# A vision tower on one Trainium2 core: other pieces for the last reads, clock-keeping products spread over the tail, patch weights centred by the vector engine, a shorter routing index

## The chip, the cores and the metric

The kernel runs on one core of one Trainium2 chip. The metric is the time of one execution on the device in microseconds (us), the median of several runs. One core has a matrix engine (PE; the loading of its stationary operand is shown as PEld), a vector engine (DVE), a scalar engine (ACT), a general engine (POOL) and a queue engine (SP), and 16 DMA engines that all queues share. Each engine executes its own instruction list in order; between engines there are only semaphores.

## The reference

16 images of 3x96x96 become 36 patches of 768 values each; with a class token there are 37 tokens an image and T = 592 tokens of width 256.

```
tokens = patches @ W.T + b                     # 768 -> 256
h  = concat([cls, tokens], axis=1) + pos
x  = layernorm(h) * g1 + b1                    # causal attention with low-rank q, k, v, out; 16 heads
h1 = h + attention(x);  a = h1 + mlp(layernorm(h1) * g2 + b2)
h  = layernorm(h + a)
logits = h @ gate.T; scores = softmax(logits); w, idx = top_k(scores, 3); w = w / sum(w)
y  = sum over the 3 chosen experts of w * fc2_e(gelu(g) * x * mult)      # 15 experts
ys = the shared expert of 512 hidden units, for every token
out = layernorm(h + y + ys)
```

A layer normalisation doesn't see a constant that is added to all features of a token, so the kernel keeps the token vectors centred (mean over the 256 features taken off).

## The kernel before, in words

Everything is float32 and features lie on partitions (2 chunks c of 128), tokens on the free axis in two halves n of 296. All orders are written out by hand: each engine has a block in which its instructions stand as they execute.

**Start.** SP issues six transfers `embed_sb<-embed` (L433), one for each chunk k of 128 of the 768 patch values; one holds the weights (`tw_sb`, 256 columns) and the patches (`pt_sb`, 576 columns). PE first multiplies zeros (`keep_clock`, `fill`: products that nobody reads, which keep it busy), then does the 24 products of the embedding into four PSUM banks. DVE adds bias and position while it takes them out into `h0` (L915). PE then multiplies `h0` by a matrix of 1/256 (`mean`, L1425), DVE subtracts those means (`centre`, L925) into `xc`, and ACT squares `xc` for the variance (`squares`, L668). `bias_means` and `centre_biases` do the same for the biases of attention output and MLP (`vec_sb`). After that PE composes the low-rank q, k and v weights (`compose`), one after the other, between the steps of the normalisation. POOL meanwhile takes the first bias row off expert weights (`less_first`, L407), which wait for their transfers, and then stages keys for the attention scores (`keys_block`, L372), for which PE waits before `scores(0)`.

**Attention, MLP.** Eight pairs of images through a software pipeline, then the low-rank MLP. The change doesn't touch them.

**Routing, during the shared expert.** The shared expert is eight units k = 0 to 7. In each, PE makes two products (`h,stage`), ACT a gelu (L821), DVE the gated product (L1336, semaphore `t1_done`), and PE two units later the down product (`xn,stage`). After its gated product of unit k DVE does a part of the routing, `routing(k)`: top 3 (`select`), places of the tokens in their experts (`order`, `slots`, from the product `positions` of PE), the chosen slots (`choose`, L1198 to L1261), one-hot tables (`groups_hot`, `places_hot`, L1281), the owners of slots (`owners`), and from PE's `slot_table` (15 products, `128x63`) the index lists for gathering and scattering (`tables`, L1301 to L1308). POOL waits for `gather_i` and then gathers token rows for 21 tiles of 128 rows (L635); PE waits for the first of them (`tile_transposed`, L1798).

**Experts and tail.** 21 tiles go through two products; POOL scatters the rows of each tile to `y_dram` (L644), a row of 1 KB each, to a place worked out from token and choice: for a group of 32 tokens the 96 rows of their three choices lie together, group after group (19 groups). When the last scatter has landed SP reads them back in five transfers (`read_rows`, L421): partition p = 32*choice + token, four groups each, one row of 1 KB for each partition and group. While this goes on, PE puts bias and residual into five PSUM banks (`b_sb,comb` and `cst_sb,hs`), then multiplies zeros 8 times, then for t = 0 to 4 waits for read t (`ld_y[t]`) and sums with the `mix` weights (`wres,embed_sb`). DVE and ACT normalise tile t (L1395 to L1408, L870, L875) and SP stores it (L532).

```
            for t in range(TT):
                pe.wait_ge(ld_y[t], 16)
                for j in range(min(PC, NSUM - PC * t)):
                    ...
```

Of the kernel before, what the change touches and what calls it, by code (L numbers as in the profile page):

```python
# [82 lines left out]
YROWS = NT * P + KS * NSUM  # L83
# [3 lines left out]
RT_END = 28  # L87
# [33 lines left out]
C_DST, C_DUMP = _col(TOPK * TT), _col(NT)  # L121
NRTE = _v


def vit_tower_kernel(nc, embed, vecs, csts, vrows, ut, out_u, out_v, fc1_u, fc1_v, fc2_u, fc2_v,
                     gate, shared, experts, mults, bias1, rtes, b2, out, comb_dram, x_dram, y_dram):
    ctx = ExitStack()
    with ctx:
# [22 lines left out]
        h0 = h0_mem[:, :].rearrange("p (c t) -> p c t", c=DC)  # L151
# [39 lines left out]
        res_b = sb("res_b", [P, DC, 2])  # L191
        w_sum = sb("w_sum", [P, 3])

# [49 lines left out]
        pick_i = sb("pick_i", [P, 2, TOPK * TT], I32)  # L243
# [24 lines left out]
        owner = pt_mem[:, 0:(NOVER) * E].rearrange("p (i e) -> p i e", e=E)  # L268
# [22 lines left out]
        def column(i):  # L291
# [6 lines left out]
        ld_emb = [sem(f"ld_emb{k}") for k in range(KP)]  # L298
        ld_cst, ld_vec, ld_out = sem("ld_cst"), sem("ld_vec"), sem("ld_out_w")
# [34 lines left out]
            sem(n) for n in ("mask_done", "pos_mm", "comb_done", "route", "hot_done", "pick_done"))  # L334
        own_done, tab_mm, tab_out, idx_done = sem("own_done"), sem("tab_mm"), sem("tab_out"), sem("idx_done")
# [20 lines left out]
        mean_mm, centred_h0, w_cen = (sem(n) for n in ("mean_mm", "centred_h0", "w_cen"))  # L356
# [74 lines left out]
        def _(sp):  # L431
            for k in range(KP):
                sp.dma_start(emb[:, k], embed[:, k]).then_inc(ld_emb[k], 16)  # L433
# [64 lines left out]
            for k in range(TOPK):  # L498
                at = NT * P + KS * (NSUM - 1) + SUMS * k
                sp.dma_start(y_dram[at + SUM_LAST:at + SUMS, :], zrow[0:SUMS - SUM_LAST, :]).then_inc(st_zero, 16)  # L500
# [163 lines left out]
        def _(act):  # L664
            def squares(ln, n, src, made, each):
                for c in range(DC):
                    act.wait_ge(made, DC * n + c + 1 if each else n + 1)
# [24 lines left out]
            squares(ln1, 0, xc[:, 0], centred_h0, False)  # L692
            squares(ln1, 1, xc[:, 1], centred_h0, False)
# [98 lines left out]
            for g in range(NH * FIC):  # L792
# [3 lines left out]
                if g == 1:  # L796
                    squares(ln2, 1, half(h1, 1), op_done, True)
                if g == 11:
                    squares(ln3, 0, half(hs, 0), mo_done, True)
            warm(ACT.Sqrt)  # L800
            squares(ln3, 1, half(hs, 1), mo_done, True)
# [1181 lines left out]
```

## Time and profile before

| what | value |
|---|---|
| median of 3 runs | 218.86 us (218.07 to 219.18) |
| the profiled execution, its own time | 218.37 us |
| its span, first to last instruction | 216.6 us |
| mean granted PE clock, share of full | 0.982 |
| PE busy | 202.2 us, 93% of the span |
| DVE, ACT, POOL busy | 106.7, 94.4, 120.4 us |
| read from memory, written | 29.25 MB, 4.06 MB |

The time is 1.8 us more than the span, for what lies before the first and after the last instruction. Busy PE time counts products in flight, so 93% doesn't mean that the array is full. In the profile "idle 0.52 <-DMA x" says that an engine stood idle for 0.52 us and that x ended it.

### The profile page before, as it was taken

To read this page: it belongs to the slowest core of one execution; us is meant where nothing else is said; L and a number is where in the kernel's file an instruction comes from. 1 tells how busy PE (TensorE), PEld (TensorE's weight loads), DVE (VectorE), ACT (ScalarE), POOL (GpSimd) and SP (SyncE) were. 2 spreads that over 40 slices of the span, in tenths; PEclk is the share of its full clock that TensorE was granted. 3 is DMA by queue.
4 is the path that set the end of the run, shared out by engine and by line. 5 is a ranking of instruction groups with operands and counts; after the bars stand their busy time and mean duration, and the time that the engine had idled before them with its cause. 6 is when DMAs were issued, how large, how long until landed. Compare 5 with 4: busy or idle time off the path is not lost.

```text
span 216.6 us, 4391 instructions
## 1 busy us (share of the span) xinstructions
PE 202.2 (93%) x1551; PEld 128.4 (59%) x1551; DVE 106.7 (49%) x295; ACT 94.4 (44%) x219; POOL 120.4 (56%) x148
## 2 busy tenths in 40 slices
PE   7999899989998899989999999899999999998952
PEld 4777577667886675756877763354444555445510
DVE  4076587748973444275579943523334222230044
ACT  2003543568868373553438672233323333324023
POOL 0040099649979867949998077407756652257000
PEclk9999999999999999999999999999999999999975
DMA  6999999920000299941021023319975321112692
GB/s 220 396 394 351 410 420 419 414 113 5 6 3 3 78 381 369 420 111 48 3 98 30 0 73 102 99 33 339 371 275 193 92 73 53 48 48 98 166 229 88
DMA packets 15054, 38.30 MB, mean 177 GB/s; under 512 B 2713, under 2 KB 6298, under 8 KB 15034
## 3 DMA queue, kind: packets, MB, share of 16 engines
q1 hardware_dynamic: 13018, 32.53, 41.7%
q0 software_dynamic: 2016, 5.51, 8.2%
q8 instruction: 13, 0.21, 0.4%
q14 instruction: 7, 0.06, 0.1%
HBM read 29.25 MB, written 4.06 MB: 154 GB/s over the span
## 4 chain that ended last, share of the span: by engine, by line
PE 81%; DVE 6%; DMA 6%; ACT 2%; issue 1%; POOL 1%; SPq 1%; POOLq 0%; DVEq 0%; ACTq 0%
PE ps L364 70%; DMA wres<-y_dram 3%; PE ps L1798 3%; PE ps L1609 2%; PE ps L1838 2%; PE ps L1622 2%; DMA embed_sb<-embed 2%; DMA y_dram<-ln_mem,dest_i 1%; PE ps L1542 1%; POOL y_dram L644 1%; DVE ln_mem L990 1%; DVE nw_i L974 1%; DVE nw L979 1%; DVE nw L980 1%; SPq L421 1%
## 5 line engine op out<-in xcount | busy, mean ns | idle before, releaser
L364 PE MATMUL ps<-wres,cT 128*64 (+1 forms) x360 | 62.9, 468 | 1.7 <-DVE cT L1363 0.6
L364 PEld LDWEIGHTS ps<-wres,cT 128*64 128x64 f32 (+1 forms) x360 | 25.5, 131 | 29.4 <-issue 22.2
L644 POOL DMA_INDIRECT y_dram<-ln_mem,dest_i x21 | 20.7, 985 | 27.3 <-ACT ln_mem L852 24.0
L407 POOL TENSOR_TENSOR wres<-wres,fac_mem 128x512 f32<-128x512 f32 x22 | 27.2, 1272 | 2.9 <-DVE ln_rs L981 2.9
L635 POOL DMA_INDIRECT embed_sb<-x_dram,gather_i x21 | 20.4, 971 | 13.5 <-DVE gather_i L1303 6.5
L1356 DVE TENSOR_TENSOR h<-ps,h 128x256 f32<-128x256 f32 x21 | 8.1, 420 | 33.0 <-PE ps L1838 24.9
L846 ACT ACTIVATE h<-ps 128x256 f32<-128x256 f32 x21 | 8.1, 384 | 30.1 <-PE ps L364 30.1
L364 PE MATMUL ps<-h,stage 128*128 128x296 f32 x64 | 18.0, 419 | 0.0
L852 ACT ACTIVATE ln_mem<-ps 128x256 f32<-128x256 f32 x21 | 8.1, 384 | 16.4 <-PE ps L364 16.4
L1363 DVE COPY cT<-ps 128x256 f32<-128x256 f32 x21 | 8.8, 423 | 10.3 <-PE ps L364 8.7
L364 PEld LDWEIGHTS ps<-h,stage 128*128 128x128 f32 x64 | 11.7, 190 | 3.7 <-issue 0.4
L553 POOL TENSOR_TENSOR wres<-wres,cst_sb 128x111 f32<-128x111 f32 x32 | 10.9, 373 | 5.1 <-PE ps L1622 5.1
L407 POOL TENSOR_TENSOR wres<-wres,hs 128x512 f32<-128x512 f32 x4 | 5.6, 1429 | 13.7 <-DMA wres<-experts 13.7
L364 PE MATMUL ps<-xn,wres 128*128 128x296 f32 x48 | 13.1, 419 | 0.0
L789 ACT ACTIVATE embed_sb<-ps,vec_sb 128x296 f32<-128x296 f32 x16 | 8.1, 505 | 10.6 <-PE ps L364 10.4
L364 PE MATMUL ps<-embed_sb 128*128 128x288 f32 (+1 forms) x63 | 12.5, 357 | 0.1
L364 PEld LDWEIGHTS ps<-embed_sb 128*128 128x128 f32 (+1 forms) x63 | 9.6, 168 | 3.3 <-DMA embed_sb<-embed 0.7
L364 PE MATMUL ps<-embed_sb,f1v 128*128 128x296 f32 x32 | 10.9, 429 | 0.6 <-DVE embed_sb L1099 0.5
L372 POOL TENSOR_TENSOR wres<-wres,cst_sb 128x148 f32<-128x148 f32 x16 | 10.2, 660 | 1.3 <-PE ps L364 1.3
L678 ACT ACT_TABLE_LOAD x8 | 10.3, 1283 | 1.2 <-DVE eps_t L887 1.1
L364 PEld LDWEIGHTS ps<-xn,wres 128*128 128x128 f32 x48 | 8.8, 190 | 3.2 <-issue 0.5
L364 PE MATMUL ps<-embed_sb,f2u 128*128 128x296 f32 x32 | 10.5, 416 | 0.0
(208 smaller groups left out, 379.4 us busy)
## 6 DMA issues: line engine op xcount, KB each, us to landing
wres<-experts SPq DMA_DIRECT2D x15, 768.0 KB, 13.4
fac_mem<-experts SPq DMA_DIRECT2D x11, 256.0 KB, 8.1
embed_sb<-embed SPq DMA_DIRECT2D x6, 416.0 KB, 5.2
wres<-ut SPq DMA_DIRECT2D x3, 768.0 KB, 8.9
stage<-shared SPq DMA_DIRECT2D x2, 771.0 KB, 16.4
wres<-y_dram SPq DMA_DIRECT2D x4, 384.0 KB, 5.7
stage<-wres SPq DMA_DIRECT2D x2, 512.0 KB
f1v<-fc_v SPq DMA_DIRECT2D x1, 512.0 KB
```

Of the source, the lines that this page charges most:

```text
L364: return nc.tensor.matmul(o, w, x, start=start, stop=stop)
L372: return eng.tensor_tensor(kblk[:, par, u, c], kT[:, c, bass.ds(p * (2 * S) + u * S, S)].unsqueeze(1).to_broadcast([P, HR, S]), cst[:, C_B ...
L407: nc.gpsimd.tensor_tensor(w1(e, c), w1(e, c), row, ALU.subtract).then_inc(less_done, 1)
L553: pool.tensor_tensor(vst[:, par, c, u].rearrange("p (r s) -> p r s", r=G3), vT[:, c, bass.ds(p * (2 * S) + u * S, S)].unsqueeze(1).to_broa ...
L635: pool.indirect_dma_start(out=xg[:, i % NXG], out_offset=None, in_=x_dram[:, :], in_offset=bass.IndirectOffsetOnAxis(ap=gather_i[:, column ...
L644: pool.indirect_dma_start(out=y_dram[:, :], out_offset=bass.IndirectOffsetOnAxis(ap=dest_i[:, column(i):column(i) + 1], axis=0), in_=ys[:, ...
L678: nc.scalar.activation(warm_t[:, i:i + 1], eps_t[:, 0:1], function)
L789: nc.scalar.activation(hm[:, f], ps[:, HM_BANK + g % 2, 0:HT], ACT.Gelu_apprx_tanh, bias=vec[:, C_FC1B + f:C_FC1B + f + 1]).then_inc(hm_do ...
L846: nc.scalar.activation(gel_r[:, i % 2], ps[:, 4 + i % 2, F:2 * F], ACT.Gelu).then_inc(ge_done, 1)
L852: nc.scalar.activation(ys[:, i % NYS], ps[:, i % 2, 0:D], ACT.Copy).then_inc(ys_done, 1)
L1356: nc.vector.tensor_tensor(a_r[:, i % 2], ps[:, 4 + i % 2, 0:F], gel_r[:, i % 2], ALU.mult).then_inc(a_done, 1)
L1363: nc.vector.tensor_copy(aT[:, i % 2].rearrange("p f s -> p (f s)"), ps[:, 2 + i % 2, 0:F]).then_inc(at_done, 1)
```

## The change

1. **Patch weights centred.** The transfer of chunk 0 is split in two (weights, then patches). DVE takes the mean over the 256 features off the weights of each chunk, in place, in two instructions (`centre_chunk`: a sum and a scaled subtraction), before PE may use the chunk (`tw_cen`). Position, class token and biases are gathered in `place_b`, centred together (`bias_means` now between chunks 3 and 4, 39 columns), and the embedding is taken out of PSUM straight into `xc`. `h0` as a result, `mean` and `centre` are gone. `squares` waits for each chunk of the half.
2. **Routing.** `choose` works on slot numbers times 64 by operations with two tensor operands and moves from unit 3 to unit 2, ahead of the gated product of unit 3; everything behind it moves a unit up. PE does `positions` before the down product of unit 0 and `slot_table` before unit 6 instead of unit 7; `tables` comes before `owners`.
3. **Last reads.** The rows of `y_dram` lie so that the 20 groups of one partition are together. Each of the five reads is now one run of 4 KB on each of 96 partitions (3 KB in the last). The places follow from two tables and a factor of 20 in `tables`.
4. **Unread products.** Instead of 8 at one place, 2 after each of the five residuals and 3 before each sum but the first.

```diff
-            for k in range(KP):
+            sp.dma_start(tw_sb[:, 0], embed[:, 0, 0:D]).then_inc(ld_emb[0], 16)
+            sp.dma_start(pt_sb[:, 0], embed[:, 0, D:EC]).then_inc(ld_pt, 16)
+            for k in range(1, KP):
                 sp.dma_start(emb[:, k], embed[:, k]).then_inc(ld_emb[k], 16)
...
+            def centre_chunk(k):
+                dve.wait_ge(ld_emb[k], 16)
+                nc.vector.tensor_reduce(tw_sum[:, k:k + 1], tw_sb[:, k], AX.X, ALU.add).then_inc(tw_cen, 1)
+                dve.wait_ge(tw_cen, 2 * k + 1)
+                nc.vector.scalar_tensor_tensor(tw_sb[:, k], tw_sum[:, k:k + 1].to_broadcast([P, D]), -1.0 / D,
+                                               tw_sb[:, k], ALU.mult, ALU.add).then_inc(tw_cen, 1)
...
-                    nc.vector.scalar_tensor_tensor(
-                        hv[:, n * HB:(n + 1) * HB, 1:S],
+                    nc.vector.tensor_tensor(
+                        by_image(xc[:, n, c])[:, :, 1:S],
                         ps[:, 2 * n + c, 0:HP].rearrange("p (b s) -> p b s", b=HB),
...
-            centre(0)
-            centre(1)
-            centre_biases()
...
-                pe.wait_ge(ld_emb[k], 16)
+                if k == KP - 2:
+                    bias_means()
+                pe.wait_ge(tw_cen, 2 * k + 2)
...
-            mean(0)
-            mean(1)
-            bias_means()
...
-                nc.vector.tensor_copy(place[:, :, :], pick_i[:, :, :]).then_inc(rt, 1)
-                nc.vector.tensor_scalar(upper[:, :], place[:, 0], NT - 0.5, float(TM), ALU.is_ge, ALU.mult).then_inc(rt, 1)
+                nc.vector.scalar_tensor_tensor(upper[:, :], pick_i[:, :], NT * TM - 0.5, tm_t[:, :],
+                                               ALU.is_ge, ALU.mult).then_inc(rt, 1)
...
                 if k == 2:
                     order()
                     slots()
+                    choose()
                 if k == 3:
-                    choose()
+                    groups_hot()
...
                 if k == 6:
-                    pe.wait_ge(rt, 9)
+                    pe.wait_ge(idx_done, 1)
+                    pe.wait_ge(tab_out, 2)
...
+        y_sums = y_dram[NT * P:YROWS, :].rearrange("(p c) d -> p c d", p=KS)
-            eng.dma_start(yr[:, lo:hi],
-                          y_dram[NT * P + KS * lo:NT * P + KS * hi, :].rearrange("(c p) d -> p c d", p=KS)) \
-                .then_inc(ld_y[t], 16)
+            eng.dma_start(yr[:, lo:hi], y_sums[:, lo:hi]).then_inc(ld_y[t], 16)
...
-            keep_clock(2, 8)
+                keep_clock(2, 2)
             pe.wait_ge(mix_done, TOPK * PC)
             for t in range(TT):
+                if t:
+                    keep_clock(2, 3)
                 pe.wait_ge(ld_y[t], 16)
```

How the instructions stand at three places. First the start of PE (all of its products go through one helper line, L364 before and L374 in the change). Before:

```order
L364 MATMUL ps<-fill 128x296 x12
L364 MATMUL ps<-embed_sb 128x288 x24
L364 MATMUL ps<-h,ones_t 128x296 x4
L364 MATMUL ps<-vec_sb,ones_t 128x2 x2
L364 MATMUL ps<-wres,cT 32x256 x12
L364 MATMUL ps<-ln_mem,ones_t 32x74 x8
```

And with the change:

```order
L374 MATMUL ps<-fill 128x296 x12
L374 MATMUL ps<-embed_sb 128x288 x16
L374 MATMUL ps<-place_b,ones_t 128x39 x2
L374 MATMUL ps<-embed_sb 128x288 x8
L374 MATMUL ps<-wres,cT 32x256 x12
L374 MATMUL ps<-ln_mem,ones_t 32x74 x8
```

The four products of 296 columns for the means are gone, and the product for the biases stands inside the embedding.

Second, PE in units 2 to 7 of the shared expert, from the product of `positions` with the triangle to the first expert tile. `mask` belongs to `positions`, `128x63` is `slot_table`. Before:

```order
L364 MATMUL ps<-xn,stage 128x296 x2
L364 MATMUL ps<-mask,tri_bf 128x90
...
L364 MATMUL ps<-xn,stage 128x296 x2
L364 MATMUL ps<-embed_sb 128x63 x15
L364 MATMUL ps<-h,stage 128x296 x4
L364 MATMUL ps<-xn,stage 128x296 x6
L1805 TENSOR_LOAD owner_i
```

With the change:

```order
L374 MATMUL ps<-mask,tri_bf 128x90
...
L374 MATMUL ps<-embed_sb 128x63 x15
L374 MATMUL ps<-h,stage 128x296 x4
L374 MATMUL ps<-xn,stage 128x296 x2
L374 MATMUL ps<-h,stage 128x296 x4
L374 MATMUL ps<-xn,stage 128x296 x6
L1833 TENSOR_LOAD owner_i
```

`positions` stands one down product earlier and `slot_table` one whole unit earlier.

Third, the end of PE: residuals, unread products (`fill`), sums. Before:

```order
L364 MATMUL ps<-b_sb,comb 80x256
L364 MATMUL ps<-cst_sb,hs 80x128 x2
L364 MATMUL ps<-fill 128x296 x8
L364 MATMUL ps<-wres,embed_sb 32x256 x18
L364 MATMUL ps<-wres,embed_sb 16x256
```

With the change:

```order
L374 MATMUL ps<-b_sb,comb 80x256
L374 MATMUL ps<-cst_sb,hs 80x128 x2
L374 MATMUL ps<-fill 128x296 x2
L374 MATMUL ps<-wres,embed_sb 32x256 x4
L374 MATMUL ps<-fill 128x296 x3
L374 MATMUL ps<-wres,embed_sb 32x256 x4
L374 MATMUL ps<-fill 128x296 x3
```

Two of the unread products stand behind each residual, and three between any two sums: 22 in place of 8.

## Rows read from the trace of the kernel before

**Rows 1.** The page, part 4: shares of the chain that ended last, by engine.

```profile
PE 81%; DVE 6%; DMA 6%; ACT 2%; issue 1%; POOL 1%; SPq 1%; POOLq 0%; DVEq 0%; ACTq 0%
```

**Rows 2.** That chain in order of time: start us, us, what.

```profile
0.72 3.54 DMA embed_sb<-embed
...
4.31 18.34 PE ps L364 x130
```

**Rows 3.** Timeline of the start, PE (each product shows as two instructions).

```profile
4.31 11.91 PE L364 MATMUL ps<-embed_sb 128*128 128x288 f32 x48
...
16.05 2.16 PE L364 MATMUL ps<-h,ones_t 128*128 128x296 f32 x8
...
18.48 1.28 PE L364 MATMUL ps<-wres,cT 128*32 128x256 f32 x18
```

**Rows 4.** Windows: from:to length, busy PE PEld DVE ACT POOL, PEclk, DMA share, GB/s.

```profile
1.50:2.65 1.15, 1.15 (x6) 0.74 (x5) 0.81 (x6) 0.89 (x1) 0.00 (x0) 1.00 0.78 124
2.65:3.60 0.95, 0.95 (x6) 0.57 (x5) 0.82 (x5) 0.00 (x0) 0.00 (x0) 1.00 0.88 312
3.60:5.00 1.40, 1.29 (x6) 0.64 (x5) 0.00 (x0) 0.00 (x0) 0.00 (x0) 1.00 1.04 418
```

**Rows 5.** Timeline, 14 to 32 us, DVE: instructions like the added ones.

```profile
14.80 1.97 DVE L915 SCALAR_TENSOR_TENSOR h<-ps,vec_sb 128x288 f32<-128x288 f32 x4 [1.17 <-PE ps L364]
...
29.07 0.40 DVE L940 TENSOR_REDUCE w_sum<-f2v 128x1 f32<-128x256 f32 x1
...
30.29 1.49 DVE L946 SCALAR_TENSOR_TENSOR f2v<-w_sum,f2v 128x256 f32<-128x256 f32 x1
```

**Rows 6.** Timeline, 27 to 38 us, what stands before `scores(0)`.

```profile
27.32 5.59 POOL L407 TENSOR_TENSOR wres<-wres,hs 128x512 f32<-128x512 f32 x4 [13.73 <-DMA wres<-experts]
...
35.40 0.96 POOL L372 TENSOR_TENSOR wres<-wres,cst_sb 128x148 f32<-128x148 f32 x2
...
38.09 0.31 PE L364 MATMUL ps<-caus_bf,ident_bf 37*37 37x296 bf16 x4
```

**Rows 7.** Timeline, 115 to 129 us, routing.

```profile
116.03 0.43 DVE L1255 CAST place<-pick_i 128x30 f32<-128x30 int32 x1
...
116.93 0.17 DVE L1260 TENSOR_TENSOR place<-place,upper 128x15 f32<-128x15 f32 x1
...
120.02 2.16 PE L364 MATMUL ps<-h,stage 128*128 128x296 f32 x8
...
120.39 1.55 DVE L1281 TENSOR_TENSOR embed_sb<-place,rte 128x640 bf16<-128x640 f32 x2
...
123.01 0.63 PE L364 MATMUL ps<-embed_sb 128*128 128x63 bf16 x15
...
124.67 1.18 POOL L635 DMA_INDIRECT embed_sb<-x_dram,gather_i  x1 [6.45 <-DVE gather_i L1303]
...
128.89 0.20 PEld L1798 LDWEIGHTS ps<-cst_sb,embed_sb 128*128 128x128 f32 x2 [0.20 <-DMA embed_sb<-x_dram,gather_i]
```

**Rows 8.** Timeline, 197 to 213 us, the tail.

```profile
197.93 0.69 PE L364 MATMUL ps<-b_sb,comb 17*128 17x256 f32 x2
...
204.08 1.17 PE L364 MATMUL ps<-fill 128*128 128x296 bf16 x8
...
205.77 0.64 PE L364 MATMUL ps<-wres,embed_sb 96*32 96x256 f32 x8 [0.52 <-DMA wres<-y_dram]
...
210.45 1.93 PE L364 MATMUL ps<-wres,embed_sb 96*32 96x256 f32 x14 [0.49 <-DMA wres<-y_dram]
...
211.23 0.25 PEld L364 LDWEIGHTS ps<-wres,embed_sb 96*32 96x32 f32 x6 [0.59 <-DMA wres<-y_dram]
...
212.46 0.42 DVE L1395 BATCH_NORM_STATS2 stats<-ps 80x6 f32<-80x256 f32 x1
```

**Rows 9.** Windows of the tail, columns as in rows 4.

```profile
202.90:210.50 7.60, 4.76 (x44) 1.99 (x46) 1.93 (x8) 1.16 (x3) 0.00 (x0) 0.90 1.02 242
209.00:210.00 1.00, 0.95 (x8) 0.07 (x7) 0.00 (x0) 0.52 (x1) 0.00 (x0) 0.50 1.12 242
```

More of the change, by code:

```diff
@@ L664, in _, with squares @@
         def _(act):
-            def squares(ln, n, src, made, each):
+            def squares(ln, n, src, made, ahead=0):
                 for c in range(DC):
-                    act.wait_ge(made, DC * n + c + 1 if each else n + 1)
+                    act.wait_ge(made, ahead + DC * n + c + 1)
                     nc.scalar.activation(sq[:, n, c], src[:, c], ACT.Square).then_inc(ln.sq, 1)
@@ L691, in _ @@
             warm(ACT.Sqrt)
-            squares(ln1, 0, xc[:, 0], centred_h0, False)
-            squares(ln1, 1, xc[:, 1], centred_h0, False)
+            squares(ln1, 0, xc[:, 0], emb_done, NH)
+            squares(ln1, 1, xc[:, 1], emb_done, NH)
             std(ln1, 0)
@@ L796, in _ @@
                 if g == 1:
-                    squares(ln2, 1, half(h1, 1), op_done, True)
+                    squares(ln2, 1, half(h1, 1), op_done)
                 if g == 11:
-                    squares(ln3, 0, half(hs, 0), mo_done, True)
+                    squares(ln3, 0, half(hs, 0), mo_done)
             warm(ACT.Sqrt)
-            squares(ln3, 1, half(hs, 1), mo_done, True)
+            squares(ln3, 1, half(hs, 1), mo_done)
             std(ln3, 1)
@@ L1316, in routing @@
                     slots()
+                    choose()
                 if k == 3:
-                    choose()
+                    groups_hot()
                 if k == 4:
-                    groups_hot()
-                    places_hot(0)
+                    for q in range(TOPK):
+                        places_hot(q)
                 if k == 5:
-                    places_hot(1)
-                    places_hot(2)
+                    tables()
                 if k == 6:
                     owners()
-                    tables()
                     softmax_start()
@@ L1423, in keep_clock, with bias_means @@
                     mm(ps[:, bank, 0:HT], fill[:, 0:P], fill[:, :])
-            def mean(n):
+            def bias_means():
+                pe.wait_ge(spread_done, 2)
+                pe.wait_ge(place_done, 3)
                 for c in range(DC):
-                    pe.wait_ge(emb_done, 2 * n + 3 + c)
-                    last = mm(ps[:, 6 + n, 0:HT], ones_d, h0[:, c, n * HT:(n + 1) * HT], c == 0, c == DC - 1)
-                last.then_inc(mean_mm, 1)
-            def bias_means():
-                for c in range(DC):
-                    last = mm(ps[:, 3, 0:2], ones_d, vec[:, C_RES + 2 * c:C_RES + 2 * c + 2], c == 0, c == DC - 1)
+                    last = mm(ps[:, 6, 0:S + 2], ones_d, place_b[:, c], c == 0, c == DC - 1)
                 last.then_inc(mean_mm, 1)
@@ L1733, in slot_table @@
                     if q == 0:
-                        pe.wait_ge(rt, 26)
-                        pe.wait_ge(t1_done, 7)
-                    last = mm(ps[:, 4, 0:3 * NT], hot[:, q],
+                        pe.wait_ge(rt, 25)
+                    last = mm(ps[:, 3, 0:3 * NT], hot[:, q],
                               hot_val[:, q].rearrange("p v i -> p (v i)"), q == 0, q == TOPK * TT - 1)
@@ L1756, in unit @@
                     pe.wait_ge(hm_done, NH * FIC)
-                if k == 3:
-                    positions()
-                if k == 7:
+                if k == 6:
                     slot_table()
```

125 lines of the change are left out of this document (75 added, 50 removed).

## Prediction, made before the changed kernel had run

> **What bounds the kernel now.** The first view to read is the chain that ended last, by engine: 81% of it is PE, 6% DVE and 6% DMA [rows 1]. So a cut counts only where PE's own work gets shorter or where PE stands still for somebody. Read in order of time [rows 2], the chain has three parts that the change touches. From 4.31 us PE runs 18.34 us in one piece, after a wait for the first embedding chunk that ends at 0.72 + 3.54 = 4.26. Here work taken from PE is time gained, as long as its inputs are there. In the middle, around 105 to 128 us, the chain is PE again and routing isn't in it. At the end PE's sums stand behind DMA waits, one for each read of `y_dram` [rows 8]. The timeline gives what stands at each place, the windows what the DMA engines moved and which clock PE had.
>
> **Start: what goes.** The means are 8 instructions; the last of them still counts as in flight when the next product starts, so I price them by the pace of the embedding, 11.91 / 48 = 0.248 each, 1.98 us in all [rows 3]. The bias product of 2 columns stays and gets 39; loading its two stationary operands takes longer than streaming either, so its growth is put at 0 (at most 4 x 39 / 296 x 0.25, 0.13). DVE's two subtractions go too, but they lie under PE's `compose`.
>
> **Start: what comes.** PE may begin chunk 0 only when DVE has centred it. By the windows 1.15 x 124 + 0.95 x 312 = 439 KB have moved by 3.60 us [rows 4], so the 426 KB of chunk 0 by 3.56, and they count as landed at 4.26: a lag of 0.7. The weights alone are 131 KB, moved by about 2.55, so landed at 3.25. The sum over 256 columns takes 0.40 as in L940. For the subtraction the rows give two ends: 0.49 (1.97 / 4, L915, 288 columns from PSUM) and 1.49 (L946, the same shape as the new one, but while POOL was at work, see the start of rows 6) [rows 5]. POOL isn't at work then (its first instruction waits for a transfer queued behind all six chunks), so I take 0.49. With three semaphore steps of 0.03 the weights are ready at 4.25, or 5.25 by the dear end. The patches are issued one DMA later and land between 4.26, as now, and half a microsecond later. So PE starts at about 4.55 instead of 4.31: 0.25 lost (0 to 1.0). Later chunks: DVE takes about 0.95 a chunk, PE 11.91 / 6 = 1.99, and by the 418 GB/s of rows 4 a chunk lands every 1.0. DVE gets ahead; its small placing instructions and PE's bias product before chunk 4 (about 12.5 us) have more than a microsecond to spare. At the dear end DVE takes 1.9 a chunk and PE walks right behind it, which costs nothing more than the 1.0. The variance gets its squares earlier and so never becomes late.
>
> **What is late next** is POOL. It stages the keys for `scores(0)` up to 35.40 + 0.96 = 36.36, and that time hangs on a transfer of expert weights, released at 27.32, not on PE [rows 6]. PE comes to `scores(0)` at 38.09, so at most 1.73 can be gained before PE waits there. 1.98 - 0.25 = 1.73 just uses that up; one more DMA in front of the queue may move the limit by 0.1 or 0.2. I take **-1.6 us** for the start (range -0.7 to -1.8). From there on the stages release each other, so the shift stays.
>
> **Routing.** An integer or one-tensor step on 15 to 30 columns took 0.43 (L1255), one with two tensors 0.17 (L1260) [rows 7]; five such steps are replaced or dropped, a good microsecond of DVE. But the gain is an index that is ready earlier: now the gather starts at 124.67, and the only wait that PE has for gathered rows is 0.20, at the second tile at 128.89. With the change `slot_table` comes before unit 6, which starts at 120.02, and the gather near 121. The danger is that DVE isn't through with the three one-hot tables by 120.0. They end at 120.39 + 1.55 = 121.94 now. `positions` comes one down product earlier (0.8), the arithmetic is 1.1 shorter, and one gated product fewer stands ahead of them (0.5): 119.6, with 0.4 to spare. PE's own work is the same, 0.63 for the 15 products moved. I take **-0.1**, from -0.3 to +0.8 (if the new integer steps cost 0.43 instead of 0.17 and PE stands at `slot_table`).
>
> **Tail, reads.** Between 202.90 and 210.50 the reads move at 242 GB/s while the DMA engines are busy all the time (share 1.02) [rows 9]. With 3.3 KB pieces they moved 418 GB/s at the same share [rows 4]. So engine time is going into pieces: a 1 KB piece occupies one engine for 16 x 1.024 / 242 = 68 ns, at 418 GB/s it would be 39. Pieces of 4 KB lie beyond the 3.3 KB ones, so I take 410 GB/s: 384 KB in 0.96 instead of 1.56 (the pace of the sums from 205.77 to 210.45, over three steps, is also 1.56 [rows 8]). The first read then lands at about 205.1 instead of 205.7, the last at about 208.8 instead of 211.2.
>
> The page "DMA: Bandwidth & Descriptors" of the Trainium skill (Specifications) puts the least size for line rate at 512 B, and its section on small descriptors gives 3 cycles of overhead for each packet beside 32 for 1 KB, 9%. By it the reads would not gain 40% but at most 9%, and the sum would come to the first rival below. The two rows above speak against it, though the reads also differ in partitions and in what lay in memory before.
>
> **Tail, PE.** PE now does five residuals from 197.93 to 204.08, then 8 unread products of 1.17 / 8 = 0.146, and waits 0.52 for the first read [rows 8]. With the change there are 2 behind each residual: 204.08 + 10 x 0.146 is 205.55 for the first sum, 0.2 earlier than before, and PE and not the DMA sets it. Then each sum is 0.64 and three unread products 0.44: 1.08 each, more than the 0.96 of the reads. The fifth sum starts at 205.55 + 4.32 = 209.9 and has 6 instructions for 8, about 0.5: 210.4. Before, the fourth and fifth sum together took 1.93 from 210.45 at a granted clock of 0.50, the lower level, 1.2 GHz [rows 8, 9]; PE had been busy for only 4.76 of 7.60 us around its fall. Now PE is busy throughout, and I expect 1.0, which is 2.4 GHz, to the end. DVE took up the last tile at 212.46; now it does at 210.5 to 210.6: **-1.9 us**. Behind it nothing changes. Ends: -0.6 if the reads keep their pace, -2.5 if the unread products fit into gaps that PE has anyway and the reads set the pace (205.1 + 4 x 0.96 + 0.9 is 209.9).
>
> **Sum.** -1.6 - 0.1 - 1.9 = -3.6 us. Against the profiled execution, 218.37, that is 214.8. That execution is 0.5 under the median of 218.86; I expect the new median to lie as far above, so **215.3 us**. About 0.5% (1.1 us, the spread of the three runs) is what a measurement can tell from no change.
>
> **Rivals.**
>
> *The size of the pieces isn't it* (chance 0.12). Something else holds the reads at 242 GB/s, and the landings stay. Then only the clock is gained: the last read lands at 211.2, its sum ends near 211.8 instead of 212.4, -0.6. In total -2.3: 216.6. For it: other partitions, fresh data; against it: the share of 1.02, which says that the engines were held, not starved.
>
> *The tail keeps PE too busy or too slow* (0.10). Changing between zeros in bf16 and sums in float32 costs gaps, as a residual hints (1.23 for two groups of at most 512 columns, where 8 instructions of a sum take 0.64), or the clock falls all the same. At 0.2 more for each of nine groups the fifth sum ends at 212.2, 0.2 before the old; in total -1.9: 217.0.
>
> *The start gains little* (0.10). DVE's subtraction costs 1.49 even with POOL idle, and the patches land late: PE starts at 5.3, and POOL's staging slips by the DMA that was added. -0.8 for the start, -2.8 in total: 216.1.
>
> *Slower: the new order in memory* (0.05). Runs of 4 KB at a step of 20 KB, 96 at a time, may collide in memory where before each transfer read one block of 384 KB; the scatters write at that step too. The price: 1.87 MB at rate r from 202.9, a lag of 0.7, 0.55 for the last sum, against 212.4 now. It decides once that eats the 1.7 of start and routing, at 9.95 us for the data or r = 188 GB/s. At 150 the data take 12.45, the last sum ends at 216.6, 4.2 later than now; net +2.5: 221.4. No row shows such a rate for large pieces; nor does one exclude it, since no transfer here has this step.
>
> The forecast itself has 0.63. Its own range is 214.2 to 216.5, from the ends of start, routing and tail, not all met at once. The first three rivals lie between 216.1 and 217.2, so 8 in 10 is held by **213.6 to 217.2**. Faster by over 0.5% (under 217.8): all but the fourth rival and the worst of the second, 0.90; within 0.5% 0.06; slower 0.04.
>
> **What would show it.** Right: PE's first `embed_sb` product at 4.4 to 4.7 and `compose` at 16.7 to 17.0; no wait over 0.3 at the staged keys; `gather_i` ready by 121 on the old scale (1.6 less in the new); reads at 380 GB/s or more; sums 1.1 apart at clock 1.0. Wrong: PE waiting for DVE at chunks 1 to 5; PE idle at `slot_table`; read rate still near 242; sums with more than 1.2 between their starts.

## The result, and the profile after

| | before | changed |
|---|---|---|
| median, same chip | 218.34 us (218.00 to 219.18, 6 runs) | 216.34 us (216.15 to 217.21, 6 runs) |
| ratio, 95% interval | | 0.9912 (0.9884 to 0.9940) |
| profiled execution, its span | 218.37, 216.6 us | 216.19, 214.4 us |
| mean granted PE clock | 0.982 | 0.994 |

The change gains 2.0 us (1.3 to 2.5 by the interval) where 3.6 were forecast. Medians and ratios, here and below, are of the executions that agree, without the few that fell in a slower state. Between the two profiled executions the gain is 2.2, and the sum below is made against these. Three numbers, all read by the same landmarks in both traces, say where it arose.

**Start: 1.34 at `compose`, 1.20 from there on.** The timeline of the changed kernel, 2 to 19 us, PE and DVE (start, length, engine, line, operation, idle time before and what ended it):

```profile
2.82 0.42 DVE L907 TENSOR_REDUCE tw_sum<-embed_sb 128x1 f32<-128x256 f32 x1 [0.27 <-DMA embed_sb<-embed]
3.28 0.42 DVE L909 SCALAR_TENSOR_TENSOR embed_sb<-tw_sum,embed_sb 128x256 f32<-128x256 f32 x1
...
4.09 8.43 PE L374 MATMUL ps<-embed_sb 128*128 128x288 f32 x32
...
5.49 0.42 DVE L907 TENSOR_REDUCE tw_sum<-embed_sb 128x1 f32<-128x256 f32 x1 [0.94 <-DMA embed_sb<-embed]
...
6.43 1.75 PEld L374 LDWEIGHTS ps<-embed_sb 128*128 128x128 f32 x8 [0.59 <-DVE embed_sb L909]
...
8.35 3.71 PEld L374 LDWEIGHTS ps<-embed_sb 128*128 128x128 f32 x16 [0.17 <-DVE embed_sb L909]
...
12.64 0.61 PE L374 MATMUL ps<-place_b,ones_t 128*128 128x39 f32 x4
...
13.08 4.13 PE L374 MATMUL ps<-embed_sb 128*128 128x288 f32 x16
...
17.14 1.28 PE L374 MATMUL ps<-wres,cT 128*32 128x256 f32 x18
```

PE starts 0.22 earlier than before and not 0.25 later, since the weights landed at 2.8 and each centring instruction took 0.42. But chunk 1 landed only at 5.49, DVE centred it, and PE's weight load waited 0.59 for that, and 0.17 more at chunk 2. `compose` starts at 17.14 where it started at 18.48 [rows 3]. The bias product takes 13.08 - 12.64 = 0.44 before the next product starts, as long as in the kernel before, where it stood ahead of `compose` (18.48 - 18.04 = 0.44):

```profile
18.04 0.50 PE L364 MATMUL ps<-vec_sb,ones_t 128*128 128x2 f32 x4
```

So the 1.34 is made up of 1.99 for the means (16.05 to 18.04 before) and 0.22 for the earlier start, less 0.72 in the 32 instructions up to the bias product (8.55 where the pace before, 11.74 / 48, gives 7.83) and 0.15 in the 16 behind it.

The same view at the first scores, 35 to 38 us:

```profile
35.88 1.67 POOL L382 TENSOR_TENSOR wres<-wres,cst_sb 128x148 f32<-128x148 f32 x4
36.84 0.13 PEld L374 LDWEIGHTS ps<-caus_bf,ident_bf 37*37 37x37 bf16 x4 [0.49 <-issue]
...
36.88 0.31 PE L374 MATMUL ps<-caus_bf,ident_bf 37*37 37x296 bf16 x4
```

From `compose` to `scores(0)` the kernel before takes 38.09 - 18.48 = 19.61 us [rows 3, 6], the changed one 19.74. POOL's four instructions on the keys run from 35.88 to 37.55, past the start of the scores, so the 0.13 may be POOL's; but the profile names no engine for it ("issue"), and in the twelve profiles of the changed kernel and its edits below the stretch is 19.61 or 19.62, once 19.70. From here the shift is constant: 1.21 at the scores, 1.20 at the first residual of the tail (196.73 for 197.93).

**Routing: nothing.** The same view, 118 to 130 us:

```profile
119.73 0.18 DVE L1332 TENSOR_TENSOR gather_i<-ps,tab 128x21 uint32<-128x21 f32 x1
...
120.21 1.17 POOL L645 DMA_INDIRECT embed_sb<-x_dram,gather_i  x1 [2.98 <-DVE gather_i L1332]
...
127.35 0.60 PE L1826 MATMUL ps<-cst_sb,embed_sb 128*128 128x128 f32 x4
128.30 1.94 PE L374 MATMUL ps<-wres,cT 128*64 x8 [0.35 <-ACT cT L849]
```

The gather starts at 120.21 for 124.67 [rows 7], 4.46 earlier, of which 3.26 are routing's own. PE's first gathered tile stands at 127.35; before it was

```profile
128.54 0.79 PE L1798 MATMUL ps<-cst_sb,embed_sb 128*128 128x128 f32 x4
```

This is 1.19 earlier: the shift of the start and no more. The 0.20 of waiting at the second tile is gone from its place, and the first product of the experts comes no sooner for it.

**Tail: 0.98.** The same view, 200 to 211 us:

```profile
200.38 2.22 SPq L431 DMA_DIRECT2D wres<-y_dram  x5
...
204.23 0.64 PE L374 MATMUL ps<-wres,embed_sb 96*32 96x256 f32 x8
...
205.56 0.16 PEld L374 LDWEIGHTS ps<-wres,embed_sb 96*32 96x32 f32 x8 [0.52 <-DMA wres<-y_dram]
...
207.05 0.16 PEld L374 LDWEIGHTS ps<-wres,embed_sb 96*32 96x32 f32 x8 [0.68 <-DMA wres<-y_dram]
...
208.54 0.16 PEld L374 LDWEIGHTS ps<-wres,embed_sb 96*32 96x32 f32 x8 [0.68 <-DMA wres<-y_dram]
...
209.59 0.63 PE L374 MATMUL ps<-wres,embed_sb 96*32 96x256 f32 x6
...
210.28 0.43 DVE L1425 BATCH_NORM_STATS2 stats<-ps 80x6 f32<-80x256 f32 x1
```

And the window over the reads, columns as in rows 4:

```profile
201.70:209.30 7.60, 6.66 (x59) 2.87 (x58) 2.42 (x11) 2.01 (x5) 0.00 (x0) 1.00 0.94 254
```

The measure that I use for the tail in all kernels is the time from SP's first issue of a read to DVE's last statistics. It is 210.28 - 200.38 = 9.90 us, where before it was 212.46 - 201.61 = 10.85, from this issue:

```profile
201.61 2.44 SPq L421 DMA_DIRECT2D wres<-y_dram  x5
```

The other 0.03 of the 0.98 lie ahead of the issue. The clock is at its upper level (1.00, 2.4 GHz) to the end, as forecast. The reads are not: 254 GB/s where 242 stood [rows 9] and 410 were forecast, and every sum but the first and last still waits for its read. The 0.95 falls into three parts, as places and not yet as causes. The first sum stands 3.85 after the issue instead of 4.16 (0.31); three steps of the sums take 4.31 instead of 4.68 (0.37); and from the fourth sum to the last statistics it is 1.74 instead of 2.01 (0.27).

The question for the experiments was therefore what holds the reads at 250, if not the size of their pieces.

### The profile page after: what moved, and what is told of

The parts are those of the page before. It is cut to its first block, busy times and chain, and to the rows that moved or that the text cites. A ratio compares the mean times of both kernels' runs of the same rounds, so it can differ in the third digit from the quotient of the medians.

```text
span 214.4 us, 4422 instructions
## 1 busy us (share of the span) xinstructions
PE 201.6 (94%) x1557; PEld 127.1 (59%) x1557; DVE 111.3 (52%) x309; ACT 94.5 (44%) x219; POOL 120.4 (56%) x148
## 4 chain that ended last, share of the span: by engine, by line
PE 81%; DVE 7%; DMA 6%; ACT 2%; issue 2%; SPq 1%; POOL 1%; POOLq 0%; DVEq 0%; ACTq 0%
PE ps L374 70%; DMA wres<-y_dram 3%; PE ps L1826 3%; PE ps L1637 2%; PE ps L1866 2%; DMA embed_sb<-embed 2%; PE ps L1650 2%; DMA y_dram<-ln_mem,dest_i 1%; PE ps L1569 1%; POOL y_dram L654 1%; DVE ln_mem L1022 1%; DVE nw_i L1006 1%; DVE nw L1011 1%; DVE nw L1012 1%; SPq L431 1%
## 5 line engine op out<-in xcount | busy, mean ns | idle before, releaser
L374 PE MATMUL ps<-wres,cT 128*64 (+1 forms) x360 | 62.9, 469 | 1.9 <-ACT cT L849 0.7
L374 PEld LDWEIGHTS ps<-wres,cT 128*64 128x64 f32 (+1 forms) x360 | 25.5, 131 | 29.9 <-issue 22.8
L374 PE MATMUL ps<-h,stage 128*128 128x296 f32 x64 | 17.9, 418 | 0.0
L374 PEld LDWEIGHTS ps<-h,stage 128*128 128x128 f32 x64 | 11.8, 190 | 3.8 <-issue 0.4
L374 PE MATMUL ps<-embed_sb 128*128 128x288 f32 (+1 forms) x63 | 13.1, 360 | 0.2
L374 PE MATMUL ps<-xn,wres 128*128 128x296 f32 x48 | 13.1, 419 | 0.0
L374 PE MATMUL ps<-embed_sb,f1v 128*128 128x296 f32 x32 | 10.9, 429 | 0.6 <-DVE embed_sb L1128 0.5
L374 PEld LDWEIGHTS ps<-embed_sb 128*128 128x128 f32 (+1 forms) x63 | 9.4, 168 | 3.5 <-DVE embed_sb L909 0.8
L374 PEld LDWEIGHTS ps<-xn,wres 128*128 128x128 f32 x48 | 8.8, 190 | 3.2 <-issue 0.5
L374 PE MATMUL ps<-embed_sb,f2u 128*128 128x296 f32 x32 | 10.5, 416 | 0.0
```

The costliest lines, as they stand in the source:

```text
L374: return nc.tensor.matmul(o, w, x, start=start, stop=stop)
```

## Experiments

All are edits of the changed kernel. "Tail" is the measure above. The changed kernel itself was profiled three times, with tails of 9.90, 9.60 and 9.59 us. Two edits below have the same number of partitions and the same sums (1 KB pieces: 9.51; no centring: 10.23), so the same tail varies by 0.7 us between single profiles.

**The order in memory alone undone.** Pieces of 1 KB, one block of 384 KB for a read, as in the kernel before; everything else of the change stays.

```diff
-        y_sums = y_dram[NT * P:YROWS, :].rearrange("(p c) d -> p c d", p=KS)
+        y_sums = y_dram[NT * P:NT * P + KS * NSUM, :].rearrange("(c p) d -> p c d", p=KS)
...
```

(The tables and the factor that give the places go back too.)

> The changed kernel with one part undone: the rows of y_dram lie as before, so each read is 1 KB a piece again. If the size of the pieces matters as I forecast, the reads fall from the changed kernel's rate to 242 GB/s and the last lands about 2 us later relative to the start of the reads. If something else holds the reads (the rival, now my theory, since the changed kernel's reads move only some 255 to 265 GB/s with 4 KB pieces), the pace between sums goes from 1.49 to at most 1.56 us and the whole is 0.2 to 0.4 us slower, 216.5 to 216.8.

Measured: 218.27 us (7 runs) beside 220.58 of the kernel before on the same chip, a slower one; ratio 0.990 (0.986 to 0.994), as large a gain as that of the whole change. The window over the reads:

```profile
202.80:209.90 7.10, 6.58 (x58) 2.77 (x57) 2.36 (x10) 1.75 (x5) 0.00 (x0) 1.00 0.98 267
```

267 GB/s in pieces of 1 KB, 254 in pieces of 4 KB, and a tail of 211.01 - 201.50 = 9.51 us. Part 3 of the change, the one that the title names first, is worth nothing that can be seen.

**The same bytes on 128 partitions.** Two kernels read 3 KB to each of 128 partitions, once as one piece, once as three of 1 KB (both are built on the old row order, and leave out that each row goes to the partition on which the sums look for it).

```diff
-            eng.dma_start(yr[:, lo:hi], y_sums[:, lo:hi]).then_inc(ld_y[t], 16)
+            at = NT * P + KS * PC * t
+            n = KS * (hi - lo)
+            cols = n * D // P
+            eng.dma_start(wres[:, PC * D * t:PC * D * t + cols],
+                          y_dram[at:at + n, :].rearrange("r d -> (r d)").rearrange("(p x) -> p x", p=P)) \
...
```

> Built on the old row order. Each of the five reads brings the same bytes, but spread over all 128 partitions, one run of 3 KB each (2.25 KB in the last), instead of 96 partitions with 4 runs of 1 KB; the sums then use wrong rows, so what is left out is the right result of the sums, at the same work. If the 96 partitions hold the reads, the rate rises to 380 GB/s or more, sums come every 1.0 to 1.1 us and the last read lands 2 us earlier. If fresh rows in memory hold them, the rate stays at 240 to 270.

> The same 128 partitions, but three runs of 1 KB for each (0.75 KB in the last); the sums use wrong rows too. With the 3 KB kernel it gives the price of the piece size by itself, with all partitions. If pieces of 1 KB cost engine time (my forecast), the rate is near 250; if only the partitions count, it is the rate of the 3 KB kernel within a tenth.

Windows of the reads, one piece of 3 KB:

```profile
205.00:206.00 1.00, 1.00 (x8) 0.59 (x6) 0.00 (x0) 0.00 (x0) 0.00 (x0) 1.00 1.02 402
206.00:207.00 1.00, 1.00 (x12) 0.37 (x11) 0.11 (x1) 0.00 (x0) 0.00 (x0) 1.00 1.05 359
```

and three pieces of 1 KB:

```profile
205.00:206.00 1.00, 1.00 (x6) 0.38 (x5) 0.00 (x0) 0.00 (x0) 0.00 (x0) 1.00 1.09 382
206.00:207.00 1.00, 1.00 (x14) 0.59 (x13) 0.00 (x0) 0.00 (x0) 0.00 (x0) 1.00 1.04 349
```

At a DMA share of 1.02 to 1.09 the engines now move 350 to 400 GB/s, in large and small pieces. In the two windows that follow it is 316 to 322 in both kernels, and over 205 to 209 us together 350 GB/s with 3 KB and 343 with 1 KB. With 3 KB the sums stand 1.05 us apart and wait for no read, and the tail is 211.08 - 202.34 = 8.74 us. With 1 KB the third read landed late and the tail was 9.99:

```profile
210.04 0.16 PEld L374 LDWEIGHTS ps<-wres,embed_sb 96*32 96x32 f32 x8 [1.49 <-DMA wres<-y_dram]
```

Each of the two was profiled once. Of the three kernels below that also bring 1 KB pieces to 128 partitions, two make PE's weight load wait for the third read as well (0.54 and 0.90 us), and neither of the two kernels that reach 350 GB/s or more with pieces of 3 or 6 KB does. Whether small pieces bring such stragglers on stays open.

**64 partitions, side by side and apart.** Is it the number of partitions, or which ones? Both kernels put 6 KB on each of 64 partitions (and leave out the same), one on partitions 0 to 63, one on every second of the 128.

```diff
+            cols = n * D // 64
+            eng.dma_start(wres[0:64, 2 * PC * D * 3 // 4 * t:2 * PC * D * 3 // 4 * t + cols],
...
+            eng.dma_start(wres[0:128:2, 2 * PC * D * 3 // 4 * t:2 * PC * D * 3 // 4 * t + cols],
...
```

(The first `dma_start` is that of one kernel, the second that of the other.)

> The reads of the tail bring the same bytes to partitions 0 to 63 only, 6 KB on each (leaves out that the rows go where the sums look for them). Theory A (the rate goes with the number of partitions written): about 64/96 of the 250 to 270 GB/s of 96 partitions, so 165 to 190 GB/s, sums 2.0 to 2.3 apart, last statistics 12 to 13 us after the issue, run 2.5 to 3 us longer than the changed kernel. Theory B (96 is slow for how its rows fall to the 16 engines, and 64, a multiple of 16 with whole rows, isn't): 320 GB/s or more.

> As the last, but to the 64 partitions 0, 2, 4 to 126 (leaves out the same). Theory A1 (what counts is the number of partitions, wherever they are): as the last, 165 to 190 GB/s. Theory A2 (what counts is how many of the four groups of 32 partitions are written, three of four for 96 partitions): 320 GB/s or more, since all four are written.

The windows of the kernel with partitions 0 to 63, the first over nearly the whole read:

```profile
204.00:212.00 8.00, 6.07 (x48) 2.60 (x47) 2.09 (x9) 1.15 (x3) 0.00 (x0) 0.93 0.99 218
206.00:207.00 1.00, 0.46 (x7) 0.17 (x9) 0.00 (x0) 0.00 (x0) 0.00 (x0) 1.00 0.99 203
207.00:208.00 1.00, 1.00 (x11) 0.25 (x8) 0.42 (x1) 0.00 (x0) 0.00 (x0) 1.00 0.99 203
```

and of the one with every second partition:

```profile
205.00:209.00 4.00, 4.00 (x40) 1.70 (x38) 1.29 (x6) 0.36 (x2) 0.00 (x0) 1.00 1.00 394
205.00:206.00 1.00, 1.00 (x7) 0.57 (x6) 0.00 (x0) 0.00 (x0) 0.00 (x0) 1.00 1.00 418
206.00:207.00 1.00, 1.00 (x13) 0.39 (x11) 0.00 (x0) 0.00 (x0) 0.00 (x0) 1.00 0.97 332
207.00:208.00 1.00, 1.00 (x15) 0.37 (x11) 0.62 (x2) 0.12 (x1) 0.00 (x0) 1.00 1.03 424
```

The means are 218 GB/s against 394, with the same bytes, the same pieces of 6 KB, the same number of partitions, both at a share of about 1.0. Second by second the first moves 264 and 252, then 203 to 215, the other 418, 332, 424 and 404. The tails are 215.39 - 202.39 = 13.00 (in the first PE's clock falls as well, to 0.50 from 211 us on) and 211.40 - 202.65 = 8.75 us. So it is neither the size of the pieces nor the number of partitions, but which of them are written: the lower half of the partitions takes about half of the full rate, every second one takes all of it. The page "SBUF — State Buffer" of the Trainium skill (Door 1: The DMA port swizzle) states why: DMAs write the 128 partitions through 16 ports, and 0 to 63 lie on eight of them. These two runs agree (203 is 0.49 of 418, and 218 is 0.55 of 394). By that rule 96 partitions side by side put two thirds of the bytes on eight ports, so at best 209 / (2/3) = 314 GB/s if eight ports take 209, the half of 418, an estimate. The three profiles of the changed kernel and that with the old order show 254 to 281 over windows of 6 to 8 us, so the rule explains most of the distance from 418, and what takes the rest stays open.

One rival is left. That the rate goes with how many of the four groups of 32 partitions are written (the second theory recorded for `e_64_apart`) gives a half, three quarters and all of it for these three layouts too, the same numbers. A read onto partitions 0 to 31 alone would tell the two apart; it wasn't run, so between them it is the page that decides and no measurement of this case.

That the partitions count could have been seen before. The loads `fac_mem<-out_u` and `fac_mem<-out_v` of the start have 96 partitions and pieces of 2 KB. In the kernel before, while they were due, the windows show

```profile
15.00:16.00 1.00, 1.00 (x6) 0.79 (x5) 1.00 (x3) 0.00 (x0) 0.00 (x0) 1.00 1.04 311
16.00:17.00 1.00, 1.00 (x5) 0.76 (x4) 0.77 (x2) 0.00 (x0) 0.00 (x0) 1.00 1.06 233
17.00:18.00 1.00, 1.00 (x5) 0.76 (x4) 0.75 (x1) 0.00 (x0) 0.00 (x0) 1.00 1.08 283
18.00:19.00 1.00, 1.00 (x17) 0.76 (x19) 0.77 (x3) 0.79 (x2) 0.00 (x0) 1.00 1.01 392
```

a dip to 233 GB/s at full share, between 418 GB/s (14 to 15 us) and 392 to 407 (18 to 20) for loads of 128 partitions. Other loads are under way in it too, so it is a hint and no measure.

**Unread products at one place.** Part 4 alone undone.

```diff
-                keep_clock(2, 2)
+            keep_clock(2, 8)
...
-                if t:
-                    keep_clock(2, 3)
```

> The changed kernel with the unread products together again, 8 behind the last residual and none between the sums. If they carry the tail's gain through the clock, the granted clock falls to 0.5 at about the third sum as before, the last two sums take about 1.9 us instead of 1.1, and the whole is 0.4 to 0.7 us slower. If the clock's fall costs nothing because the reads set the pace, within 0.1 us.

Measured: 218.21 us (6 runs), ratio 0.989 (0.985 to 0.993). No difference in the median is shown: the ratio of the changed kernel, from another chip, was 0.991. The tail is 212.34 - 202.21 = 10.13 us, inside the 9.51 to 10.23 above. Its profile does show the part at work: reads at 266 GB/s in the window over them, a first sum 3.87 after the issue as in the changed kernel, and then

```profile
210.00:211.00 1.00, 0.59 (x8) 0.16 (x8) 0.56 (x4) 0.63 (x2) 0.00 (x0) 0.87 0.64 188
211.00:212.00 1.00, 1.00 (x10) 0.19 (x6) 0.66 (x3) 0.25 (x2) 0.00 (x0) 0.50 0.06 16
```

the clock falls to its lower level (0.50, 1.2 GHz) shortly before 211, after stretches in which PE was busy for 0.6 of the time. From the fourth sum to the last statistics it takes 212.34 - 210.41 = 1.93 us, with the products spread 1.74 or 1.75, in all five profiles that have them. The spreading is worth 0.2 us by this, less than a median of six runs can show.

**No centring after chunk 0.** DVE centres one chunk, PE takes the others as they land (leaves out most of the centring). Run beside the changed kernel on one chip.

```diff
+                if k:
+                    return
                 dve.wait_ge(ld_emb[k], 16)
...
-                pe.wait_ge(tw_cen, 2 * k + 2)
+                if k:
+                    pe.wait_ge(ld_emb[k], 16)
+                else:
+                    pe.wait_ge(tw_cen, 2)
```

> DVE centres the patch weights of chunk 0 alone; chunks 1 to 5 go to PE as they landed (leaves out most of the centring). Theory A (PE's waits at chunks 1 and 2 are the centring, 0.85 us behind the landing): no wait there, compose 0.4 to 0.6 earlier than in the changed kernel, near 16.6. The scores of the first pair then stay near 36.8, because POOL's staged keys end where they end, so the total gains at most 0.1. Theory B (the waits are the landing of the chunks): PE still waits at chunk 1, compose less than 0.2 earlier. Theory C (POOL doesn't hold the scores): they come 0.4 earlier as well and the total with them.

> The changed kernel unchanged, on the chip of the three runs beside it, so that they can be compared with it and not only with the kernel before. Expected: about 2 us under the kernel before, ratio 0.988 to 0.994; first sum about 7.5 us after the issue of the last reads, read windows at 250 to 270 GB/s.

The changed kernel took 216.31 us there, ratio 0.991 (0.987 to 0.994). Its first sum came 3.84 us after the issue of the reads, and 7.50 after the first residual; the 7.5 expected above fits only this second count. Over the reads the window showed 281 GB/s, more than expected. Without the centring PE's embedding, from its first product to `compose`, takes 16.83 - 4.19 = 12.64 us, with it 13.05 in the first profile and 13.20 in the second: the centring of chunks 1 and 2 costs PE 0.4 to 0.6. The scores follow 19.62 behind `compose`, at 36.45, 0.63 earlier than in the second profile. POOL's expert weights, which were to hold them near 36.8, had landed 0.68 earlier too (27.18 for 27.86), so that this run doesn't show where POOL's limit lies. The total was 216.11 in one run, no gain that can be told: the tail took 10.23 instead of 9.60, its reads waited for longer.

**All rows on 128 partitions, for real.** If partitions are what counts, rows can be laid out so that each read brings the three rows of 128 tokens to 128 partitions, and a tile is summed by three products with 128x128 weights.

```diff
-                for j in range(min(PC, NSUM - PC * t)):
-                    last = mm(ps[SUMS * j:SUMS * j + rows, SUM_BANK[t], 0:D], mix[:, j, t, 0:rows], yr[:, PC * t + j], ...)
+                for k in range(TOPK):
+                    last = mm(ps[0:rows, SUM_BANK[t], 0:D], mix[0:rows, k, t, 0:rows], yr[0:rows, t, k], ...)
```

> The same result as the changed kernel, but a read of the tail now brings the three rows of each of 128 tokens to 128 partitions (3 runs of 1 KB on each; y_dram laid out choice by choice) instead of 96 partitions with four rows. A tile is then summed by 3 products of 128x128 weights instead of 4 of 96x32. Theory A (the number of partitions sets the rate, the size of the runs doesn't): reads at 320 to 400 GB/s, sums about 1.1 apart and set by PE, last DVE statistics at most 9.2 us after the issue of the reads, where the changed kernel needs 9.9, so 0.7 to 1.2 us faster than the changed kernel on the same chip. Theory B (runs of 1 KB are slow; the two wide kernels before were fast for another reason, such as rows that a scatter had left nearby): reads at 240 to 270 GB/s, sums 1.5 apart, no gain. A straggling read, as in the wide kernel with 1 KB runs, would cost 1.2 of it.

> As the last, and POOL stages the first keys before it takes the bias row off the third block of expert weights. If POOL holds the scores of the first pair of images, they come 0.1 us earlier (that is what PE stood idle there) and nothing else moves; PE's compose limits the rest. If POOL has slack there, no difference from the last kernel. Either way within 0.3 us of it.

Measured: 218.97 and 218.28 us, ratios 1.001 (0.999 to 1.004) and 1.001 (0.999 to 1.003): the whole gain is gone. The timeline of the second (`c_wide_keys`), PE, 204 to 209 us, says why:

```profile
204.14 1.46 PE L374 MATMUL ps<-wres,embed_sb 128*128 128x256 f32 x6
...
205.43 0.54 PE L374 MATMUL ps<-fill 128*128 128x296 bf16 x3
...
205.81 1.46 PE L374 MATMUL ps<-wres,embed_sb 128*128 128x256 f32 x6
```

The reads move 324 GB/s (202 to 207 us) and in this profile no sum waits for one any more (in `c_wide` the third waited 0.54), but a sum takes 1.46 us: 6 instructions, 0.24 each. The changed kernel's 8 instructions with 96x32 weights take 0.64, 0.08 each, though each passes the same 256 columns. The reading that fits is that its four products, which write four different groups of 32 columns, pass side by side, while three of 128 columns follow each other. Sums stand 1.67 apart and the tail is 212.33 - 200.35 = 11.98 (12.43 in `c_wide`). A faster transfer was bought with a slower sum. As to the keys staged earlier: it is 19.62 from `compose` to scores, and 19.61 in `c_wide` without that, so the move shows nothing about POOL; the difference of the two medians is within their intervals.

**128 partitions and sums of 32 columns.** The rows as in the kernel before, but 384 of them as three columns of 128 partitions, and six products of 128x32 (with zeros where a row belongs to another group), one unread product between sums, and a clearing of the weights by DVE.

```diff
-                    last = mm(ps[SUMS * j:SUMS * j + rows, SUM_BANK[t], 0:D], mix[:, j, t, 0:rows], yr[:, PC * t + j],
-                              False, True)
+                    for c in range(TOPK):
+                        if (j, c) in mix_of:
+                            last = mm(..., mix[:, mix_of[j, c], t, 0:rows], yr[:, TOPK * t + c], ...)
```

> The same result as the changed kernel. The rows lie in memory as in the kernel before (96 for each group of 32 tokens), but a read takes 384 of them as three columns of 128 partitions, so all partitions are written; a tile is then summed by 6 products of 128x32 weights (4 column groups, zeros where a row belongs to another group) in place of 4 of 96x32, with 1 unread product instead of 3 between sums, and DVE clears the weights first. Theory A (partitions set the rate of the reads, and 32-column groups side by side keep the sums cheap, unlike the 128x128 weights of the wide kernel): reads at 320 to 400 GB/s, 6 products 0.8 to 1.0 us, sums 1.1 to 1.3 apart, last DVE statistics 8.8 to 9.3 us after the issue of the reads (9.6 and 9.9 in the two profiles of the changed kernel), 0.4 to 1.0 us faster than it, ratio to before 0.986 to 0.989. Theory B: 6 products cost as much as in the wide kernel (1.46 a tile), sums 1.5 apart, no gain.

Measured: 217.44 us (6 runs) beside 221.36 of the kernel before, ratio 0.981 (0.978 to 0.985), on the slower chip. This is the best ratio of all, better than the 0.986 to 0.989 expected, and 0.8 us below the two kernels timed on that chip earlier. But its profile, of the slowest of its runs (219.0), doesn't say that the tail did it: a sum of twelve instructions takes 1.07 (0.09 each, near the 0.08 of 96x32 weights), the third waited 0.70 for a read, and the tail is 213.08 - 202.38 = 10.70 where 8.8 to 9.3 were expected. Reads were at 347 GB/s in the mean from 204 to 209 us. Where the better median comes from stays open.

**The changed kernel a third time.**

> The changed kernel unchanged once more, for how much its time and the landing of its last reads vary from chip to chip: the kernel before took 221.3 us on one chip and 218.4 on the others. If the ratio to the kernel before holds, it is 0.988 to 0.994 on any chip. On the chip of 221.3 us it may be lower, 0.983 to 0.990 (217.6 to 219.2 us), since the kernel before lost more to the granted clock there (mean 0.985, with the lower level at its end) than the changed one would. The kernel that reads onto 128 partitions and sums with 6 products of 128x32 had 217.44 us there, and should be 0.4 to 1.0 below this one.

216.56 us beside 219.21, ratio 0.988 (0.985 to 0.991). It ran on the same chip as the second, not on the slow one, so the comparison with the last kernel wasn't had. Its profile shows how much the start varies: PE's first product waited 0.95 for the patches and came at 5.14, `compose` at 19.06, later than in the profile of the kernel before. On the slow chip the kernel needed 1.3 to 2.2 us more than on the others between the first scores and the issue of the reads, in each profile of seven different edits; that is why tails, and not totals, are compared above.

## Why the prediction was right or wrong

**Right in kind.** Faster, 216.34 us, inside the range of 213.6 to 217.2. It also lies inside the forecast's own 214.2 to 216.5, but of the 3.6 us forecast only 2.0 came. The forecast value of 215.3 was 1.0 us too low, because the first rival held: the size of the pieces isn't it. Its 216.6 was 0.3 from the result, in part by luck: it counted 0.4 too much for the start (-1.6) and 0.4 too little for the tail (-0.6). Three things that the prediction had listed as signs of being wrong were seen: PE waited for DVE at chunks 1 and 2, the reads stayed near 242 GB/s, and sums stood 1.33 to 1.49 apart where they waited for a read.

**Start, forecast -1.6, measured -1.2.** The removal of the means counted as worked out; DVE's price was at the cheap end, 0.42 an instruction. The step that failed is "DVE gets ahead": the landing of a chunk every 1.0 us was taken to begin at once behind chunk 0, but chunk 1 landed at 5.49, 1.4 after the patches of chunk 0, and PE, which had started early, stood 0.59 + 0.17 for DVE. The run without centring prices this at 0.4 to 0.6. The bias product didn't grow (0.44 before and after), as said. POOL as the next limit was foreseen; at most the 0.13 before the scores are its. How much of the 1.2 is the change and how much the landing of that execution, the other profiles tell: from PE's first product to `compose` it was 14.17 us before, and with centring 12.83 to 13.37 in eleven profiles and 13.92 in the third of the changed kernel. So, whenever PE starts, this stretch is shorter by 0.8 to 1.3, once by 0.25, than in the single profile of the kernel before. No run undid part 1 or part 2 alone.

**Routing, forecast -0.1, measured 0.** DVE was through with its tables in time and `gather_i` came at 119.73, as said (by 121 less the shift). That the gather starts 4.46 earlier changes nothing, since PE's list and not the gather decides when the first expert tile begins.

**Tail, forecast -1.9, measured -0.98.** The failed step is "engine time is going into pieces": the share of 1.02 at 242 GB/s was read as engine time spent on each piece, and the 418 GB/s of 128 partitions was taken as the rate of larger pieces. But the share was 0.99 to 1.00 at 203 GB/s as well as at 418, so a full share doesn't say what the engines are held by. The reads came at 267 GB/s with pieces of 1 KB and at 254 to 281 with 4 KB, so larger pieces gave nothing that can be told. Had they come at 400, the rest of the working would have held: with 3 KB on 128 partitions the tail is 8.74 us, with sums 1.05 apart, and the prediction's own line (sums 1.08 apart, last statistics at 210.5 to 210.6 after an issue at 201.61) is 8.9 to 9.0. The clock was right, and worth 0.2 to 0.3 instead of up to 0.6. For the other 0.68 of the tail (0.31 at the first sum, 0.37 over three steps) no cause is shown. Nothing of it belongs to the order in memory, as the run with the old order shows (3.89 for three steps, where the changed kernel has 4.31, 4.01 and 3.96). Nor does it come from the spreading of the unread products: with them together the first sum stands 3.87 after the issue and three steps take 4.33, where the kernel before has 4.16 and 4.68. It may be that the single profile of the kernel before, with 242 GB/s, was at the slow end of what executions vary in; it was not profiled again, and no run undid parts 3 and 4 at once.

**The other rivals.** PE wasn't too busy in the tail: the gaps around the unread products stayed within what was allowed for (1.05 to 1.06 from sum to sum where no read is waited for). Memory didn't collide: 254 to 281 GB/s at a step of 20 KB, 267 without it.

## What to carry to other kernels

Don't carry a DMA rate from one part of a trace to another unless the same partitions are written: compare transfers that agree in partitions before you blame the size of pieces, and look at both halves. When a full DMA share goes with a low rate, ask what the engines wait for. And before making a transfer wider, price what the consumer pays for the new layout: here the wide read by itself brought the tail from 9.5 to 10.2 us down to 8.7, and the wide sums took it up to 12.0.

## What the runs showed of the hardware beyond that

- Sixty-four partitions at a step of two took 394 GB/s over four microseconds, 64 side by side 218 over eight. So a transfer to half of the partitions had the full rate when it was spread.
- Pieces of 1 KB and of 4 KB moved to 96 partitions at rates that can't be told apart (242 and 267 GB/s; 252 to 281).
- The landing of the first chunks varies by a microsecond between executions of the same kernel (PE's first product at 4.09, 4.27 and 5.14), as much as the gain of the start itself.
